# Softmax score tiles in a retention and attention block: from two bank pairs for score rows to three single banks each for rows and columns

## What is computed

```python
scores = jnp.einsum('bhqd,bhkd->bhqk', q, k) / np.sqrt(HEAD_DIM)
bias = rel_bias[bucket_ids]                # by key minus query
attn = jax.nn.softmax(scores + bias[None], axis=-1)
out = jnp.einsum('bhqk,bhkd->bhqd', attn, v)
return jnp.einsum('blc,dc->bld', out.transpose(0, 2, 1, 3).reshape(Bx, Lx, C), wo) + bo
```

## Time and profile before

| | |
|---|---|
| median of 3 executions | 3271.77 us (3270.47 to 3277.3) |
| the profiled execution | 3276.13 us |
| its span in the trace | 3274.3 us |
| granted TensorE clock, mean | 0.952 of full |
| busy: PE, DVE, ACT, POOL | 93%, 62%, 53%, 38% of the span |
| chain of waits, largest lines | PE L727 18%, PE L781 18%, PE L545 11%, PE L758 9% |

### The profile page before, as it was taken

The page is one execution under the profiler, slowest core; times in us unless marked ns, Lnnn a source line. Parts: engine busy times, 40 slices in busy tenths (PEclk is TensorE's granted clock), DMA queues, the critical chain, the costliest instruction groups (busy, mean ns, idle before and its releaser), DMA issues.

```text
span 3274.3 us, 50455 instructions
## 1 busy us (share of the span) xinstructions
PE 3029.7 (93%) x18786; PEld 1607.8 (49%) x18786; DVE 2018.4 (62%) x3231; ACT 1729.9 (53%) x3667; POOL 1252.6 (38%) x1764
## 2 busy tenths in 40 slices
PE   5989999899998999989998899998999989999997
PEld 3634456444664446644465444653446534465344
DVE  4458635685457854578445784457834678346882
ACT  2428734377344763448633475435754358533674
POOL 2324433254333443334433344333443334433453
PEclk8979999799998999989999899998999989999899
DMA  6050000500014000140002300023000320004100
GB/s 166 1 116 2 2 1 15 115 15 2 1 22 107 15 1 1 34 96 15 1 1 52 78 15 1 1 69 61 15 1 1 91 39 15 1 1 103 28 2 14
DMA packets 54771, 107.52 MB, mean 33 GB/s; under 512 B 12400, under 2 KB 34976, under 8 KB 54400
## 3 DMA queue, kind: packets, MB, share of 16 engines
q1 hardware_dynamic: 54272, 104.22, 14.1%
q10 hardware_dynamic: 256, 0.07, 0.0%
HBM read 56.66 MB, written 36.72 MB: 29 GB/s over the span
## 4 chain that ended last, share of the span: by engine, by line
PE 76%; DVE 6%; DMA 5%; SPq 4%; issue 4%; POOL 3%; ACT 3%; ACTq 1%; POOLq 0%; DVEq 0%
PE psum L727 18%; PE psum L781 18%; PE psum L545 11%; PE psum L758 9%; PE psum L832 3%; SPq L440 3%; DMA SQ<-mrow 2%; PE psum L580 2%; PE psum L881 2%; PE psum L813 2%; PE psum L867 2%; DMA parts<-mixed 2%; PE psum L884 2%; DVE mx L1446 1%; PE psum L616 1%
## 5 line engine op out<-in xcount | busy, mean ns | idle before, releaser
L1446 DVE TENSOR_REDUCE mx<-psum 128x1 f32<-128x1024 f32 x1024 | 1238.1, 1223 | 295.8 <-PE psum L727 295.0
L1190 ACT ACTIVATE Z<-psum 128x512 f32<-128x512 f32 x2048 | 1115.4, 597 | 426.0 <-PE psum L758 386.6
L1639 POOL TENSOR_TENSOR Z<-Z,band_exp 128x256 f32<-128x256 f32 (+1 forms) x1152 | 713.8, 640 | 920.2 <-ACT Z L1190 912.5
L758 PE MATMUL psum<-SQ,SK 64*128 64x512 f32 x2048 | 885.4, 481 | 53.9 <-DMA SQ<-mrow 53.9
L727 PE MATMUL psum<-SK,SQ 63*128 63x512 f32 x2048 | 792.8, 475 | 41.3 <-issue 21.4
L781 PE MATMUL psum<-Z,Vx 128*17 128x256 f32 x8192 | 643.5, 389 | 0.0
L727 PEld LDWEIGHTS psum<-SK,SQ 63*128 63x128 f32 x2048 | 326.0, 199 | 449.8 <-issue 320.9
L758 PEld LDWEIGHTS psum<-SQ,SK 64*128 64x128 f32 x2048 | 368.2, 189 | 251.1 <-ACT Z L1190 178.5
L545 PE MATMUL psum<-Wqkvg,Z 128*128 128x512 f32 x768 | 380.2, 620 | 18.7 <-ACT Z L1085 18.7
L781 PEld LDWEIGHTS psum<-Z,Vx 128*17 128x17 f32 x8192 | 138.9, 96 | 291.5 <-issue 275.3
L1584 POOL TENSOR_TENSOR Z<-Z 128x512 f32<-128x512 f32 x64 | 81.1, 1267 | 358.9 <-DVE Z L1369 358.9
(11 more groups left out here) (120 smaller groups left out, 3227.7 us busy)
## 6 DMA issues: line engine op xcount, KB each, us to landing
parts<-Z SPq DMA_DIRECT2D x32, 512.0 KB
X<-L_attn_a_x SPq DMA_DIRECT2D x8, 1024.0 KB, 5.5
SQ<-parts SPq DMA_DIRECT2D x32, 256.0 KB, 7.4
SK<-parts SPq DMA_DIRECT2D x32, 256.0 KB, 10.1
SQ<-parts SPq DMA_DIRECT2D x16, 512.0 KB, 8.2
SK<-parts SPq DMA_DIRECT2D x16, 512.0 KB, 12.9
out<-X SPq DMA_DIRECT2D x16, 512.0 KB, 19.7
SQ<-mixed SPq DMA_DIRECT2D x96, 64.0 KB, 2.3
```

The lines of the kernel that those rows point to most:

```text
L758: pe.matmul(col_bank(s, i), SK[rows_of(h), h // 2, j * P:j * P + P], SQ[rows_of(h), h // 2, 512 * half:512 * half + 512], start=True, stop ...
L1190: nc.scalar.activation(ring[:, n % RING, :], col_bank(s, i), ACT.Exp)\
L1446: nc.vector.tensor_reduce(mx[:, blk, col:col + 1], bank_pair[u % 2], AX_X, ALU.max)\
L1639: nc.gpsimd.tensor_tensor(ring[:, n % RING, a:z], ring[:, n % RING, a:z], band_exp[:, 4 * hg + COLS[i], at:at + z - a], ALU.mult)\
```

## The change

The score rows get banks 0, 1 and 2 in turn, one tile of 512 keys each (`row_bank`), and each is reduced by itself: `row_max` makes two reductions into `mx2`, and after the sixteenth unit of a block a third kind of reduction joins the halves of the block into `mx`, counted by the new tally `mx_f`. It waits for the last half on its own engine, and `max_transpose` waits for it. A score row tile waits for the reduction of the tile three before. The score columns get banks 3, 4 and 5 in turn in all steps, and tile n waits for the exponential of tile n-3. `WIDE` goes. The output projection gets other banks (`W_IN` and `W_OUT`), and what begins in banks 0 and 1 of the next batch waits for `attention_out` of pair 1 (`x_att` at 2).

```diff
--- before.py
+++ after.py
@@ -98,7 +98,6 @@
 
         psum = ctx.enter_context(nc.psum_tensor("psum", [P, 8, 512], F32))
         bank = [psum[:, i, :] for i in range(8)]
-        bank_pair = [psum[:, 2 * i:2 * i + 2, :].rearrange("p a n -> p (a n)") for i in range(2)]
 
 
         ident = sb("ident", [P, P])
@@ -147,6 +146,7 @@
         oarg = sb("oarg", [P, 4])
         ors = sb("ors", [P, 2, 4])
         mx = sb("mx", [P, 8, 16])
+        mx2 = sb("mx2", [P, 2, 16, 2])
         mrow = sb("mrow", [16, 2, P], F32R)
         orc = sb("orc", [P, 4, 4])
 
@@ -269,8 +269,9 @@
         spread = [None] + [tally("sp", f"spread{share}", 8, 16) for share in (1, 2)]
         p_vx = tally("pe", "p_vx", 4)
         vx_cp = tally("act", "vx_cp", 4)
-        mx_s = tally("pe", "mx_s", NU)
-        mx_r = tally("dve", "mx_r", NU)
+        mx_s = tally("pe", "mx_s", 2 * NU)
+        mx_r = tally("dve", "mx_r", 2 * NU)
+        mx_f = tally("dve", "mx_f", 8)
         mx_tp = tally("pe", "mx_tp", 8)
         mx_row = tally("act", "mx_row", 8)
         mx_in = [tally("sp", f"mx_in{i}", 16, 16) for i in range(2)]
@@ -339,15 +340,20 @@
             return hg, half, KEY_ORDER[half][s % 8]
 
 
-        WIDE = range(units.index(NU) + 1, NS - 4)
-
-        W_BANKS = (0, 2, 2, 6)
+        ROWS_END = units.index(NU) + 1
+
+        W_IN = (0, 2, 2, 6)
+        W_OUT = (1, 0, 3, 7)
         LN_BANK = (0, 0, 0, 0, 4, 4)
         K_BANK = (2, 2, 6, 6)
 
-        def col_bank(s, i):
-
-            return bank[(4, 5, 2, 3)[i] if s in WIDE else 4 + i % 2]
+        def row_bank(c):
+
+            return bank[c % 3]
+
+        def col_bank(n):
+
+            return bank[3 + n % 3]
 
         def sum_bank(k):
 
@@ -529,7 +535,7 @@
                 need(pe, z_norm, b, t + 1)
                 if t == 0:
 
-                    need(pe, w_T_early, b - 1, 1)
+                    need(pe, x_att, b - 1, 2)
                 else:
 
 
@@ -712,26 +718,25 @@
                 for share in (1, 2):
                     if u == NT * SHARES[share].start:
                         need(pe, spread[share], b, 8)
-                if u < 2:
-
-                    reach(pe, fn_T, 2 * norm_at(b, 3) + 2)
-                    need(pe, c_lo, b, 8)
-                else:
-                    need(pe, mx_r, b, u - 1)
-
             def score_rows(b, u, k):
 
                 h, i, _, _ = unit(u)
+                c = 2 * u + k
                 if k == 0:
                     rows_wait(b, u)
-                mm = pe.matmul(bank[2 * (u % 2) + k], SQ[rows_of(h, MAX_ROW), h // 2, i * P:i * P + P],
-                               SK[rows_of(h, MAX_ROW), h // 2, 512 * k:512 * k + 512], start=True, stop=True)
-                if k == 1:
-                    mm.then_inc(mx_s.sem, 1)
+                if c == 0:
+                    reach(pe, fn_T, 2 * norm_at(b, 3) + 2)
+                elif c == 2:
+                    need(pe, c_lo, b, 8)
+                elif c > 2:
+                    need(pe, mx_r, b, c - 2)
+                pe.matmul(row_bank(c), SQ[rows_of(h, MAX_ROW), h // 2, i * P:i * P + P],
+                          SK[rows_of(h, MAX_ROW), h // 2, 512 * k:512 * k + 512], start=True, stop=True)\
+                    .then_inc(mx_s.sem, 1)
 
             def max_transpose(b, blk):
 
-                need(pe, mx_r, b, 16 * blk + 16)
+                need(pe, mx_f, b, blk + 1)
                 if blk < 2:
                     reach(pe, kv_r, 2 * (mix_at(b - 1, 3) if b > 0 else mix_at(b, 1)) + 2)
                 else:
@@ -744,18 +749,14 @@
                 n = 4 * s + i
                 if i == 0 and s % 8 == 0:
                     need(pe, mx_in[(s // 8) % 2], b, 4 * (s // 16 + 1))
-                if n < 2:
+                if n < 3:
                     need(pe, vx_cp, b, 4)
                     if b > 0:
                         reach(pe, r_tanh, 2 * mix_at(b - 1, 3) + 2)
-                elif s == WIDE.start and i >= 2:
-                    need(pe, mx_r, b, NU)
-                elif s in WIDE and s > WIDE.start:
-                    need(pe, e_p, b, n - 3)
                 else:
-                    need(pe, e_p, b, n - 1)
+                    need(pe, e_p, b, n - 2)
                 h = 4 * hg + COLS[i]
-                pe.matmul(col_bank(s, i), SK[rows_of(h), h // 2, j * P:j * P + P],
+                pe.matmul(col_bank(n), SK[rows_of(h), h // 2, j * P:j * P + P],
                           SQ[rows_of(h), h // 2, 512 * half:512 * half + 512],
                           start=True, stop=True).then_inc(e_s.sem, 1)
 
@@ -795,22 +796,22 @@
                 need(pe, o_n, b, 7 + pr // 2)
 
                 if pr == 0:
-                    need(pe, mx_r, b, NU)
-                elif pr == 1:
-                    need(pe, e_p, b, 4 * WIDE.stop)
+                    need(pe, mx_r, b, 2 * NU)
                 elif pr == 2:
                     need(pe, x_att, b, 2)
                 for i in range(2):
                     for c in range(C):
-                        mm = pe.transpose(bank[W_BANKS[pr]][:, (2 * i + c) * P:(2 * i + c) * P + P],
+                        mm = pe.transpose(bank[W_IN[pr]][:, (2 * i + c) * P:(2 * i + c) * P + P],
                                           aO[:, 2 * pr + i, c * P:c * P + P], ident[:, :])
                 mm.then_inc(w_tp.sem, 1)
 
             def w_project(b, pr):
                 need(pe, *((w_T_early, b, pr + 1) if pr < 2 else (w_T, b, pr - 1)))
+                if pr == 2:
+                    need(pe, e_p, b, 4 * NS)
                 for i in range(2):
                     for c in range(C):
-                        mm = pe.matmul(bank[W_BANKS[pr] + 1][:, i * D:i * D + D],
+                        mm = pe.matmul(bank[W_OUT[pr]][:, i * D:i * D + D],
                                        aT[:, pr % 2, (2 * i + c) * P:(2 * i + c) * P + P],
                                        WT[:, A_O, c, :], start=c == 0, stop=c == C - 1)
                 mm.then_inc(p_wo.sem, 1)
@@ -836,7 +837,7 @@
             def first_projects(b):
 
                 need(pe, z_T, b, 2)
-                need(pe, x_att, b - 1, 1)
+                need(pe, x_att, b - 1, 2)
                 project(b, 0, 0, 0, p_qk)
                 project(b, 0, 1, 512, p_v)
 
@@ -1170,7 +1171,7 @@
 
                     need(act, w_tp, b, pr + 1)
                     need(act, p_wo, b, pr - 1)
-                    nc.scalar.copy(aT[:, pr % 2, :], bank[W_BANKS[pr]]).then_inc(w_T.sem, 1)
+                    nc.scalar.copy(aT[:, pr % 2, :], bank[W_IN[pr]]).then_inc(w_T.sem, 1)
 
                 if b > 0:
                     last_mix(b - 1)
@@ -1187,7 +1188,7 @@
                     for i in range(4):
                         n = 4 * s + i
                         need(act, e_s, b, n + 1)
-                        nc.scalar.activation(ring[:, n % RING, :], col_bank(s, i), ACT.Exp)\
+                        nc.scalar.activation(ring[:, n % RING, :], col_bank(n), ACT.Exp)\
                             .then_inc(e_p.sem, 1)
                         if i == 3 and block_before(s) is not None:
                             max_rows(block_before(s))
@@ -1442,16 +1443,20 @@
 
                 def row_max(u):
                     _, _, blk, col = unit(u)
-                    need(dve, mx_s, b, u + 1)
-                    nc.vector.tensor_reduce(mx[:, blk, col:col + 1], bank_pair[u % 2], AX_X, ALU.max)\
-                        .then_inc(mx_r.sem, 1)
+                    for k in range(2):
+                        need(dve, mx_s, b, 2 * u + k + 1)
+                        nc.vector.tensor_reduce(mx2[:, blk % 2, col, k:k + 1], row_bank(2 * u + k), AX_X, ALU.max)\
+                            .then_inc(mx_r.sem, 1)
+                    if u % 16 == 15:
+                        need(dve, mx_r, b, 2 * u + 2)
+                        nc.vector.tensor_reduce(mx[:, blk, :], mx2[:, blk % 2], AX_X, ALU.max).then_inc(mx_f.sem, 1)
 
                 def attention_out(pr):
 
                     need(dve, p_wo, b, pr + 1)
                     need(dve, x_cb, b, pr + 1)
                     xs = X_of[b % 2][:, 2 * pr:2 * pr + 2, :].rearrange("p t n -> p (t n)")
-                    nc.vector.tensor_tensor(xs, bank[W_BANKS[pr] + 1], xs, ALU.add).then_inc(x_att.sem, 1)
+                    nc.vector.tensor_tensor(xs, bank[W_OUT[pr]], xs, ALU.add).then_inc(x_att.sem, 1)
 
                 for u in range(AHEAD):
                     row_max(u)
@@ -1490,7 +1495,7 @@
                             ins_ = nc.vector.tensor_tensor(dst[:, i], o[:, i, :, 0:HD],
                                                            orc[:, i, :].unsqueeze(2).to_broadcast([P, 4, HD]), ALU.mult)
                         ins_.then_inc(o_n.sem, 1)
-                    if s == WIDE.start + 1 and b + 1 < B:
+                    if s == ROWS_END + 1 and b + 1 < B:
                         ln1_stats(b + 1)
                     if s == 58:
                         need(dve, e_pv, b, 56)
@@ -1499,7 +1504,7 @@
                     if s == NS - 4:
```

(2 more changed lines are left out.)

## The result

The changed kernel takes 3166.33 us (3162.94 to 3172.75, 4 executions) against 3273.23 (3270.47 to 3277.3): a ratio of 0.9675, 95% interval 0.9654 to 0.9696. That is 107 us less. The prediction was 3178, 94 less, with a range of 3140 to 3243. The profiled execution took 3172.75, its span is 3171.0, 103.3 shorter than that of before, and the mean granted clock is 0.956.

The account below looks back on a forecast made before the run. The ring of two column banks between PE and ACT was taken as the bound, DVE close behind. Savings of 0.9 + 9.8 + 1.1 = 11.8 us a batch, 94 in all, gave 3178 us, range 3140 to 3243.

Parts of the forecast that it names:

- The bound before: Attention steps: the ring of column tile, two exponentials, column tile sets the pace, 2.73 us a step, DVE 0.28 us behind.
- Reductions of 512: Score row maxima on DVE: 0.60 us each in a row, four a step 2.40 us against PE's 2.44.
- The join: Once a block on DVE, joining the halves of the maxima: 0.25 us, between 0.15 and 0.45.
- What PE loses to DVE: Row tiles waiting for DVE: PE stops about 0.5 us per normalization and 0.3 per join; a block takes 21.1 us.
- The stretch at full clock: Half-steps from the clock's rise to the end of the rows: 130.0 us a batch instead of 139.8, 9.8 less.
- First steps: Four half-steps without `weigh` at the low clock: pace 1.2 us instead of 1.51, 1.25 less, counted as 0.9 a batch.
- Last steps: Steps 60 to 63: 2.44 us a step instead of 2.72 with three column banks, 1.1 us less a batch.
- Before step 0: Score rows between the channel mix's matmuls, three row banks instead of four: counted as nothing, bounds 0 to 1.5 us.
- (1): Rival: a block's maxima land late, each of 56 blocks waits 0.4 us, 22 in all, 3200 us; chance 0.12.
- (2): Rival: reductions of 512 overlap less than copies, 0.65 us each, 22.3 us a block, 3242 us; chance 0.10.
- (3): Rival: successive reductions do not overlap, 0.69 us each, DVE becomes the bound, 23.65 us a block, slower at 3306; chance 0.08.
- (4): Rival: DVE's events cost PE nothing, the stretch is 125.2 us, 38 less than forecast, 3140 us; chance 0.06.

Follow-up runs that it names:

- experiment 1: Changed kernel with score columns back in two banks, tile n waiting for exponential n-2: 3306.0 us, ratio 1.0102 against the kernel before.
- experiment 3: Changed kernel with the second reduction reading 256 of its 512 columns, leaving out keys 768 to 1023: 3141.5 us, ratio 0.960 against the kernel before.
- experiment 4: Changed kernel with the four multiplications of an output's normalization made one instruction: 3158.0 us, ratio 0.9654 against the kernel before.
- experiment 6: Changed kernel with each block's join one reduction later on DVE: 3164.5 us, ratio 0.9677 against the kernel before.
- experiment 7: Changed kernel with four score row banks instead of three before step 0: 3159.5 us, ratio 0.966 against the kernel before.
- experiment 5: Changed kernel with the maxima's transposition, copy and four DMAs one step later for blocks 1 to 7: 3343.0 us, ratio 1.0227 against the kernel before.
- experiment 2: Changed kernel with score rows in two single banks, tile c waiting for reduction c-2: 3355.8 us, ratio 1.0254 against the kernel before.

## Why the prediction was right

**The bound before.** That the ring of two column banks set the old pace is what experiment 1 shows: with the third bank taken away, and nothing else, the waits, a step of 2.75 us and the late rise of the clock come back.

**Reductions of 512** was the term that decides. 0.60 us was taken from a copy of the same size; 24 in a row take 0.61 each. The Trainium skill's 120 cycles plus elements ("VectorE: DVE Perf Modes", the section on the TRN2 errata), 0.66 us by the estimate, does not agree with the 0.61 of this trace for reductions that follow one another. (The prediction's 0.69 for one copy alone stands in none of its rows; the trace of before has 0.68 to 0.69.) "DVE is no bound by itself, by a hair" was the wrong side of the hair: at 0.61, four are 2.44 a step, the same as PE, and the two events a block then fall to DVE's account. Experiments 3, 4 and 6 show it as the bound: what DVE is spared comes off the block. The sum was not hurt, since both ways give 21.1 us: 8 x 2.44 plus PE's events, or 32 x 0.61 + 0.81 + 0.22 + 0.52 for DVE. That the two ways agree is luck, as is the forecast of a block to 0.01 us; the prediction had the right waits, and the wrong engine as the one that is never idle.

**The join** was taken as 0.25 and costs 0.22, of which experiment 6 takes 0.17 away. **What PE loses to DVE**: 0.5 a normalization forecast, 0.52 measured; 0.3 a join forecast, 0.21 measured; a block 21.1 forecast, 21.09 measured. The stretch at full clock, forecast 9.8 us a batch shorter, is 9.6 shorter; the forecast's own numbers give that too, for 99 x 1.22 is 120.8 and not 120.5, and 1042.0 to 1181.9 is 139.9 and not 139.8.

**First steps** is the term that was mis-sized: 0.9 us a batch forecast, 2.8 measured in the mean. Two parts of it failed. The first is "DVE's two reductions make the new pace 1.2": the four half-steps without `weigh` took 1.06 us each, which is 1.84 us saved and not 1.25. Two reductions take 1.22; the row banks stood free when the steps began, so the row tiles could run up to three ahead of DVE. (No edit tests that.) The second is "the clock rises near 1042", by which the prediction took some of the gain away again: it took the rise as fixed in time. In fact the first `weigh` at the full clock came 2.0 to 6.1 us earlier after the first column tile, in every batch, and with two column banks it was late again (experiment 1). So instead of losing 0.35 us the batch gained another 1.0.

**Last steps**: 1.1 forecast; steps 60 to 63 give 1.0, the whole last stretch 1.2. **Before step 0** was priced at nothing with 1.5 as a bound; it is 0.9 in the mean of the profiled execution, a good part of it from the first batch (36.6 us, where the kernel before and all but one of the experiments have 28.6 to 33.9), and experiment 7 puts 0.8 on the bank.

**The sum.** Between the profiled executions it is 103 us and not 94: the first steps give 15 more than forecast, the full-clock stretch 2 less, the last steps 1 more, the stretch before step 0 takes 7, and the rest gives 2. So the total is as near as it is because an error of 15 us met one of 7 the other way. The 107 us between the medians are nearly 4 more, which the scatter of the executions covers.

**The rivals.** (1) falls by experiment 5: 1.0 us to spare. (2) and (3) fall by the 0.61 of DVE's row, and by the block. (4) falls by the late row tile at 1062.70 (0.52 us) and by the block of 21.09.

## What to carry to other kernels

A ring of two buffers between two engines makes each wait for the other whenever one item's way there and back is longer than two items' work; a third buffer takes it away, and where PSUM is full, halving what one item needs can free it. Then cost the halves: here a reduction that stood ready behind another took 1.13 us for 1024 columns and 0.61 for 512, so a fixed part of about 0.1 us (2 x 0.61 - 1.13), where the lengths of single ones (1.22 and 0.68) give 0.14. Read it from rows of operations that follow one another. When three engines are within a few per cent, expect the bound to move to the next one and price what it does beside the main loop (here a normalization and a join a block), for that is where the next gain is.

## What the runs showed of the hardware that was not expected

After the stop before step 0 the clock rose sooner where PE's half-steps were shorter. The first `weigh` at full speed begins 5.3 to 9.3 us after the first column tile in the changed kernel, whose half-steps before it take 1.06 us, and 10.8 to 13.2 us after it in the kernel before, where they take 1.51, with the same matmuls, in 8 batches of each. It does not go with the number of column banks: experiment 2, with three of them but half-steps of 1.4 us, has 9.2 to 13.4 us, much like experiment 1 with two. But the pace isn't all of it. With the same 1.06 us three batches reach 11.2 us (two in experiment 6, one in experiment 5), and one in experiment 7, whose first half-steps take 1.07, 11.3, so the ranges overlap, though the means of 8 batches don't: 6.0 to 8.6 us in the seven kernels with the short half-steps, 11.3 to 11.9 in the three others. What decides in a single batch stays open.

And the clock can fall again after a short stop: in experiment 5 a stop of PE of 1.40 us (1.74 in one batch) before block 7, where PE goes on without score rows, was followed by 24 to 31 us at 1.2 GHz in 6 of 8 batches, and by none in the other two. The changed kernel, without the stop, kept 2.4 GHz there in all 8. So a chain that is late by 1.3 us in a block cost 177 us between the medians, where 56 such waits are 73.
